# A fused involution and mixture-of-experts kernel on one core: the last group's routing done in a row, and the last scatters put behind the additions

## The chip, the cores and the metric

The kernel runs on one core of one Trainium2 chip. The metric is the time of one execution in device microseconds (us); lower is better. The engines are TensorE (PE, with its weight loads PEld), VectorE (DVE), ScalarE (ACT), GpSimd (POOL) and SyncE (SP, which here only issues transfers). Each works through its own list of instructions strictly in the order in which they are written, and waits on semaphores where the program says so.

## The reference

```python
x = x + conv(_ln_c(x))            # x: 4 x 128 x 56 x 56
#   h    = reduce_w @ x + reduce_b       (128 -> 32 channels)
#   kern = span_w @ h + span_b           (49 taps x 16 groups, each pixel has its own)
#   conv = sum over 49 taps of kern * shifted x
t = tokens of x                   # 12544 tokens of 128 channels
t = t + ffn(_ln_t(t))
#   probs = softmax(t @ router_w.T), the best 2 of 8 experts, their shares made to sum to 1
#   y_e   = w2[e] @ (silu(w1[e] @ t) * (w3[e] @ t))      128 -> 341 -> 128
#   ffn   = sum over a token's 2 experts of share * y_e
```

## The kernel before, in words

The work has two halves that overlap. The **convolution** runs over 28 tiles of 448 pixels (8 image rows), each in 25 steps of one or two taps: TensorE makes the per-pixel kernels in `kern_ps` (L586), VectorE multiplies them with the shifted input (L851), and GpSimd (L1088) and TensorE (L601) add up the products. The **experts' half** takes finished tokens. Tiles are gathered in 15 groups (two tiles each, then tile 26 alone and tile 27 alone). For a group, VectorE does the `route` (19 small operations: best two experts, shares), TensorE the `rank` (running counts, L564 and L567), VectorE the `place` (4 operations: each token's row, `slots`) and the `table` (16 operations: which expert and rows each block of 512 tokens has). GpSimd then scatters each token's row twice into `xs` in DRAM, in order of experts: 8 indirect transfers per tile (L1097). When all scatters of a group have landed, the group's **blocks** of 512 rows can be loaded. There are 56 blocks. Block b needs: a load of its rows `xb` (L485) and of its expert's weights (L494, L499) from SyncE; a transpose X(b) on TensorE (L573), copied out by ScalarE and VectorE; six matmul slots of the hidden layer (L623, L624, L627), with silu on ScalarE and a product `hid` on VectorE; three thirds of the second layer (L536, 24 matmuls in all), called y(b) here; a copy `y_tok` on ScalarE (L685); and four indirect **additions** into `out` by GpSimd (L1109). The first addition of a block waits until all four of the block before have landed (`s_add`), since two blocks may hold the same token.

What sets the order is a table of numbers worked out when the program is built. Each engine's code is a loop over steps S, and a step number says in which step each piece of work stands. The convolution ends at S = 700; blocks 31 to 55 are added after it. A group's routing is written as offsets from `ROUTER_AT[g]` (for the last group, 700): `ROUTE_OFF`, `RANK_OFF`, `PLACE_OFF`, `TABLE_OFF`. The scatters stand in `SCATTER_AT`, behind each other, during the convolution only in the steps of a tile that `SCATTER_J` lists, and after it one in every step. A group's blocks may start at `READY` (its last scatter's step plus `LANDING`, 5 steps). From `READY` follow the steps of the slots, of X (`X_AT`), of y (`Y_AT`), of the loads (`LOAD_AT`) and of the additions (`ADD_AT`). The PSUM tile `bank` is shared by X, y, the router's logits and the rank, one use after another in order of their steps, so a use that waits holds up all uses behind it. Blocks 35 to 37 are those of the group of tiles 24 and 25, 38 and 39 those of tile 26, and 40 to 55 those of tile 27. The first load of a group (block 35, 38 or 40) waits for the group's last scatter to have landed (L478), and block 40's also for the eight `pad` transfers (L466), which fill each expert's last block with empty rows.

The load of a block and the wait of the group's first block:

```python
if b == BLOCK0[g]:
    sp.wait_ge(s_tab, TABLES.index(g) + 1)
    ...
        sp.wait_ge(s_scat[i], 16 * 2 * SUBS * tiles)
    if g == NG - 1:
        sp.wait_ge(s_pad, 16 * EXPERTS)
```

Of the kernel before, what the change touches and what calls it, by code (L numbers as in the profile page):

```python
# [23 lines left out]
TILES = B * PER_IMG  # L24
# [17 lines left out]
LATE = 8  # L42
# [34 lines left out]
CONV_END = TILES * TAPS  # L77
# [5 lines left out]
LANDING = 5  # L83


def at(p, j):
    return p * TAPS + j
# [3 lines left out]
J_STAT1, J_RSTD1, J_NORM1, J_XN, J_H = 0, 4, 6, 9, 21  # L91

PIECE_J = (3, 4, 5, 7, 8, 10, 12)
SCATTER_J = [(1, 5, 9, 11, 13, 15, 17, 19, 21, 23) if t < LATE else (1, 4, 7, 10, 13, 16, 19, 22, 24) for t in range(TILES)]
ADD_J = (0, 2, 5, 8, 11, 14, 17, 20, 23)


ROUTE_OFF = (19, 19, 19, 21, 21, 21, 21, 23, 23, 23, 25, 25, 25, 29, 29, 31, 31, 31, 31)
RANK_OFF = 26
PLACE_OFF = (27, 27, 29, 29)  # L100
TABLE_OFF = (33, 33, 33, 35, 35, 35, 35, 37, 37, 37, 37, 39, 39, 39, 41, 41)
EXP_OFF, GATES_OFF = 24, 32

ROUTER_AT = [at(tiles[-1] + 1, 0) for tiles in GROUPS_OF]
SCATTER_AT = {}
READY = []
_free = FIRST
for _g, _tiles in enumerate(GROUPS_OF):
    _S = max(_free, ROUTER_AT[_g] + PLACE_OFF[-1] + 1)
    _items = [(t, q, k) for t in _tiles for q in range(SUBS) for k in range(2)]  # L110
    while _items:
        if _S >= CONV_END or _S % TAPS in SCATTER_J[_S // TAPS]:
            SCATTER_AT[_S] = _items.pop(0)
        _S += 1
    _free = _S
    READY.append(max(_S + LANDING, ROUTER_AT[_g] + TABLE_OFF[-1] + 4))

SLOT_AT = []
_S, _acc = 0, 0
for _b in range(NBLOCKS):  # L120
    _S = max(_S, READY[BATCH_OF[_b]] + 7)
# [11 lines left out]


TAKEN = {at(_t - 1, j) for _t in range(TILES) for j in (J_XN, J_H)} | {at(_t + 1, j) for _t in range(TILES) for j in (J_XN2, J_LG)}
TAKEN |= {S + RANK_OFF for S in ROUTER_AT}

X_AT, Y_AT, LOAD_AT, ADD_AT = {}, {}, {}, {}
_x = []
for _b in range(NBLOCKS):  # L140
    _ready = READY[BATCH_OF[_b]]
    _S = max(_ready + 3, SLOT_AT[(_b - 2) * SLOTS + 5] if _b >= 2 else 0)
    if _b < 2:
        _S = max(_S, SLOT_AT[_b * SLOTS] - 4)
# [8 lines left out]
    _n = 3 if _y < CONV_END else 1  # L153
# [3 lines left out]
    assert _y not in Y_AT and (not _b or _y > _x[-1][1])  # L157
    Y_AT[_y] = _b
    _x.append((_S, _y))
_add = 0  # L160
for _b in range(NBLOCKS):
    _ready = READY[BATCH_OF[_b]]
    LOAD_AT.setdefault(max(_ready - 2, _x[_b][0] - 8), []).append(("x", _b))
    LOAD_AT.setdefault(max(_ready - 1, SLOT_AT[(_b - 2) * SLOTS + 5] + 1 if _b >= 2 else 0), []).append(("w", _b))
    LOAD_AT.setdefault(max(_ready, _x[_b - 2][1] + 1 if _b >= 2 else 0), []).append(("w2", _b))
    for _q in range(BSUBS):
        _add = max(_add, _x[_b][1] + 2)
        while _add < CONV_END and (_add % TAPS not in ADD_J or _add in ADD_AT):
# [15 lines left out]
    BANK_AT.setdefault(_S, []).append(("y", _b))  # L184

for _g in range(NG):
    BANK_AT.setdefault(ROUTER_AT[_g] + RANK_OFF, []).append(("rank", _g))
BANK_NO = {}
for _S in sorted(BANK_AT):
    for _use in BANK_AT[_S]:  # L190
# [24 lines left out]
for _t in range(TILES):  # L215
    _S = at(_t, J_X1 + 1)
# [21 lines left out]
def build(nc, x, w_red, b_red, w_span, router, w13, w2, ident, lower, consts, tabs, ids, empty, out):  # L238
    with ExitStack() as ctx:  # L239
# [190 lines left out]
        def _(sp):  # L430
# [70 lines left out]
            for S in range(FIRST, END):  # L501
                p, j = divmod(S, TAPS)
                if j == 12 and p >= 0 and p < WPIECES:
                    load_raw(p)
                if j == 20 and p >= 0 and p < WPIECES:
                    store_w(p)
                if j == J_X1 + 1 and 1 <= p <= TILES:
                    t = p - 1
                    sp.wait_ge(s_x1, t + 1)
                    sp.dma_start(token_rows(out, t), x1[:, t % 3]).then_inc(s_spill[t % 3], 16)  # L510
                    if t + 4 < TILES:
                        sp.dma_start(xt[:, t % 4], token_rows(x, t + 4)).then_inc(s_xin[t % 4], 16)
                if S == ROUTER_AT[NG - 1] + TABLE_OFF[-1] + 1:
                    pad()
                for what, b in LOAD_AT.get(S, []):
                    load_block(what, b)
# [131 lines left out]
        def _(act):  # L648
# [115 lines left out]
            for S in range(FIRST, END):  # L764
                p, j = divmod(S, TAPS)
                if p == -1 and j in PIECE_J:
                    i = PIECE_J.index(j)
                    act.wait_ge(s_span_in[i], 16)
                    act_f(span[:, i * SCOLS:(i + 1) * SCOLS], prod[0:98, i, 0:SCOLS], ACT.Copy).then_inc(s_piece_hi, 1)
                if j == 14 and 0 <= p < WPIECES:  # L770
                    act.wait_ge(s_wraw_in, 16 * (p + 1))
                    if p >= 2:
                        act.wait_ge(s_wstore, 16 * (p - 1))
                    act_f(wb[:, p % 2, :, 0, :], w_raw[:], ACT.Copy).then_inc(s_whi, 1)
                if S in MOE_AT and MOE_AT[S] % 2 == 0:
# [12 lines left out]
                if J_NORM1 <= j < J_NORM1 + 2 and p + 1 < TILES:
                    normalise("ln1", p + 1, j - J_NORM1)
                if J_NORM2 <= j < J_NORM2 + 2 and 0 <= p - 1 < TILES:  # L790
                    normalise("ln2", p - 1, j - J_NORM2)
                if j == J_NORM2 + 4 and 0 <= p - 1 < TILES:
                    twin(p - 1)
                for g in range(NG):
                    if S == ROUTER_AT[g] + EXP_OFF:
                        exponentials(g)
                    if S == ROUTER_AT[g] + GATES_OFF:
                        gates(g)

        @block.vector  # L800
        def _(dve):
# [204 lines left out]

            def routing(S):
                for g in range(NG):
                    for k, off in enumerate(ROUTE_OFF):
                        if S == ROUTER_AT[g] + off:  # L1010
                            route(g, k)
                    for k, off in enumerate(PLACE_OFF):
                        if S == ROUTER_AT[g] + off:
                            place(g, k)
                    for k, off in enumerate(TABLE_OFF):
                        if BATCH[g] and S == ROUTER_AT[g] + off:
                            table(g, k)

            def hidden(n):
# [6 lines left out]
            for S in range(FIRST, END):  # L1026
# [20 lines left out]
                if j == J_X1 and 0 <= p - 1 < TILES:  # L1047
                    t = p - 1
# [12 lines left out]
        def _(pool):  # L1061
# [121 lines left out]
```

## Time and profile before

| | |
|---|---|
| median of 3 runs | 1503.39 us (1500.45 to 1503.68) |
| the profiled execution, its own time | 1498.94 us |
| its span, first to last instruction | 1497.1 us |
| busy: PE, PEld, DVE, ACT, POOL | 1243.9, 1015.6, 1122.8, 579.5, 1112.2 us |
| mean granted clock of TensorE | 0.95 of full speed |

Busy time is the sum of an engine's instructions; an engine can be waited for without being busy, and a busy one need not be waited for. The shares are means over a convolution of some 1200 us and a stretch behind it of some 290 us, which have different limits; the change is about the passage from one to the other. The times in the rows below are us from the span's start.

### The profile page before, as it was taken

What the parts mean: (1) busy time and instruction counts of PE and PEld (TensorE: products, weight loads), DVE (VectorE), ACT (ScalarE), POOL (GpSimd) and SP (SyncE); (2) the same over time, 40 slices, a digit from 0 to 9 for tenths busy, and PEclk for the clock granted to TensorE, in tenths of its full rate; (3) what the DMA queues carried; (4) which work ended last, traced back from release to release, by engine and by line L of the source; (5) the groups of instructions that cost most, each with busy time, mean ns of one, the idle gap of its engine ahead of it and who ended that gap; (6) DMA issues with size and microseconds to landing.
All of it is one profiled execution on the core that took longest, in us unless ns stands there. A gap on an engine that the chain in (4) does not pass through costs nothing. (4 is left out here: it accounts for less than half of the span.)

```text
span 1497.1 us, 23125 instructions
## 1 busy us (share of the span) xinstructions
PE 1243.9 (83%) x7667; PEld 1015.6 (68%) x7667; DVE 1122.8 (75%) x1663; ACT 579.5 (39%) x1960; POOL 1112.2 (74%) x788
## 2 busy tenths in 40 slices
PE   4898878788988989899899898899989887587771
PEld 2676767676766777677787777777778676465661
DVE  5998888988898998888889898888889943222220
ACT  4333333334443444444345343454434244133230
POOL 4787979784686887678788687877778875665665
PEclk9999898998999999999999999999999999899996
DMA  4111111112232242332324232243322445666652
GB/s 124 41 60 48 59 49 59 49 31 88 53 79 60 69 97 63 88 78 60 85 59 103 62 86 62 60 100 83 71 58 48 105 119 129 174 137 134 145 117 25
DMA packets 93346, 120.40 MB, mean 80 GB/s; under 512 B 11531, under 2 KB 72428, under 8 KB 93082
## 3 DMA queue, kind: packets, MB, share of 16 engines
q1 hardware_dynamic: 53802, 90.97, 20.0%
q0 software_dynamic: 39424, 27.96, 13.3%
q8 instruction: 61, 1.00, 0.3%
q14 instruction: 59, 0.48, 0.1%
HBM read 78.92 MB, written 42.65 MB: 81 GB/s over the span
## 5 line engine op out<-in xcount | busy, mean ns | idle before, releaser
L851 DVE TENSOR_TENSOR prod<-kern_ps,xn 128x896 f32<-128x896 f32 x592 | 627.9, 1082 | 65.7 <-PE kern_ps L586 63.2
L586 PE MATMUL kern_ps<-h_stack,span 98*128 98x448 f32 x1372 | 466.3, 426 | 112.7 <-DVE prod L851 72.1
L1088 POOL TENSOR_TENSOR acc_p<-acc_p,prod 128x896 f32<-128x896 f32 x192 | 435.9, 2270 | 74.1 <-DVE prod L851 69.4
L1109 POOL DMA_INDIRECT out<-y_tok,idx x224 | 351.6, 1570 | 137.4 <-issue 66.2
L601 PE MATMUL acc_ps<-ident_sb,prod 128*112 128x128 f32 x2864 | 388.4, 280 | 0.0
L601 PEld LDWEIGHTS acc_ps<-ident_sb,prod 128*112 128x112 f32 x2864 | 341.3, 137 | 37.9 <-DVE x L1053 7.8
L586 PEld LDWEIGHTS kern_ps<-h_stack,span 98*128 98x128 f32 x1372 | 227.1, 200 | 205.5 <-DVE prod L851 121.5
L1097 POOL DMA_INDIRECT xs<-rows_x,slots x224 | 219.0, 978 | 61.0 <-issue 41.3
L536 PEld LDWEIGHTS bank<-w2b,hid 114*128 114x128 f32 x1344 | 181.7, 202 | 50.7 <-DVE xf_lo L1046 26.0
L536 PE MATMUL bank<-w2b,hid 114*128 114x128 f32 x1344 | 190.1, 288 | 26.2 <-DVE xf_lo L1046 15.9
L780 ACT ACTIVATE silu<-h_ps 114x512 f32<-114x512 f32 x132 | 79.0, 598 | 235.0 <-PE h_ps L627 235.0
L1024 DVE TENSOR_TENSOR hid<-silu,h_ps 114x512 f32<-114x512 f32 x132 | 89.9, 681 | 97.9 <-ACT silu L780 68.8
L623 PE MATMUL h_ps<-xf_hi,wb 128*114 128x512 f32 x264 | 118.5, 449 | 15.3 <-ACT silu L780 13.6
L1084 POOL TENSOR_TENSOR acc_p<-prod 128x896 f32<-128x896 f32 x28 | 62.9, 2247 | 85.9 <-DVE prod L851 52.2
L685 ACT ACTIVATE y_tok<-bank,xb 128x128 f32<-128x128 f32 x224 | 64.1, 373 | 118.6 <-PE bank L536 98.1
L627 PE MATMUL h_ps<-xf_lo,wb 128*114 128x512 f32 x264 | 106.1, 402 | 0.0
L624 PE MATMUL h_ps<-xf_hi,wb 128*114 128x512 f32 x264 | 105.9, 401 | 0.0
L845 DVE TENSOR_TENSOR kern_ps<-kern_ps,xn 128x896 f32<-128x896 f32 x80 | 87.2, 1090 | 12.3 <-PE kern_ps L586 11.4
L848 DVE TENSOR_TENSOR prod<-kern_ps,prod 128x896 f32<-128x896 f32 x80 | 87.3, 1091 | 2.8
L1024 DVE TENSOR_TENSOR hid<-silu,kern_ps 114x512 f32<-114x512 f32 x36 | 24.7, 685 | 84.2 <-ACT silu L780 63.1
L1074 POOL TENSOR_TENSOR rstd_ln<-veps_ln,minus_half 112x4 f32<-112x4 f32 x56 | 67.0, 1196 | 15.0 <-ACT veps_ln L718 14.9
L755 ACT ACTIVATE rows_x<-x,shift_ln,rstd_ln 112x128 f32<-112x128 f32 x112 | 47.8, 485 | 56.4 <-POOL shift_ln L1076 56.3
(154 smaller groups left out, 1349.9 us busy)
## 6 DMA issues: line engine op xcount, KB each, us to landing
wb<-wexp SPq DMA_DIRECT2D x56, 684.0 KB, 5.4
xb<-xs SPq DMA_DIRECT2D x56, 264.0 KB, 3.0
w2b<-in_w SPq DMA_DIRECT2D x56, 171.0 KB
xt<-in_x SPq DMA_DIRECT2D x28, 224.0 KB, 3.4
out<-x SPq DMA_DIRECT2D x28, 224.0 KB, 2.6
wexp<-wb SPq DMA_DIRECT2D x8, 684.0 KB, 3.2
xs<-rows_x,slots POOLq DMA_INDIRECT x224, 2.3
out<-y_tok,idx POOLq DMA_INDIRECT x224
```

The lines of the kernel that those rows point to most:

```text
L536: i = mm(bank[:, k * C:(k + 1) * C], hid[:, (CPE * b + c) % HR, k * 128:(k + 1) * 128], w2b[:, b % 2, c, :], start=c == 0 and k == 0, stop ...
L586: last = mm(kern_ps[:, g % 2, i, 0:N], span[:, k * C:(k + 1) * C], h_stack[:, t % 2, :], start=True, stop=True)
L601: last = mm(acc_ps[0:SUB, k * C:(k + 1) * C], src[:, at_:at_ + SUB], ident_sb[:], is_transpose=True, start=u == BY_PE[t][0] and i == 0 and ...
L623: mm(ps, lo, xf_hi[:, b % 2, :], start=True, stop=False)
L624: mm(ps, hi, xf_hi[:, b % 2, :], start=False, stop=False)
L627: mm(ps, hi, xf_lo[:, b % 2, :], start=False, stop=True).then_inc(done, 1)
L848: v.tensor_tensor(dst.rearrange("p (i n) -> p i n", i=2), kern, prod[:, (g - 1) % PRING, :].rearrange("p (i n) -> p i n", i=2), ALU.add).t ...
L851: v.tensor_tensor(pair_rows(dst), kern.rearrange("p i (r w) -> p i r w", w=W), taps, ALU.mult).then_inc(s_prod, 1)
L1024: v.tensor_tensor(hid[:, n % HR, :], silu[:, n % 2, :], h_at(n, 1), ALU.mult).then_inc(s_hid, 1)
L1088: g_.tensor_tensor(acc_p[:], acc_p[:], prod[:, (t * TAPS + u) % PRING, :], ALU.add).then_inc(s_padd, 1)
L1097: g_.indirect_dma_start(out=xs, out_offset=bass.IndirectOffsetOnAxis(ap=slots[:, k, n:n + 1], axis=0), in_=rows_x[:, t % XN2RING, q, k, :] ...
L1109: g_.indirect_dma_start(out=out, out_offset=bass.IndirectOffsetOnAxis(ap=idx[:, b % XBRING, q:q + 1], axis=0), in_=y_tok[:, b % 2, q * C:( ...
```

## The change

It has four parts. The last group (tile 27) gets a table of offsets of its own, `LAST_OFF`: route at steps 718 and 720, rank and exponentials at 719, place at 720, gates and table at 721, where before they stood between 719 and 741. In the last tile of the convolution scatters may stand in 12 steps instead of 9. The scatters that are left at step 700 (22; before, 25) lose their own steps and are issued behind the fourth addition of blocks 31 to 37, by `SCATTERS_BEHIND`; the plan's `READY` is still worked out from their former steps, so the blocks move up: X(38) from step 732 to 729, X(40) from 748 to 741, the program's end from 855 to 851. A load of `xb` now keeps its order, and the first one of a late group is planned 4 steps ahead of X instead of 8. The eight pads move from step 742 to 722.

```diff
-SCATTER_J = [(1, 5, 9, 11, 13, 15, 17, 19, 21, 23) if t < LATE else (1, 4, 7, 10, 13, 16, 19, 22, 24) for t in range(TILES)]
+SCATTER_J = [(1, 5, 9, 11, 13, 15, 17, 19, 21, 23) if t < LATE else (1, 4, 7, 10, 13, 16, 19, 22, 24) if t < TILES - 1 else
+             (1, 4, 6, 9, 10, 12, 15, 16, 18, 19, 22, 24) for t in range(TILES)]
...
+LAST_OFF = {"route": (18,) * 13 + (20,) * 6, "rank": 19, "exp": 19, "place": (20,) * 4, "gates": 21, "table": (21,) * 16}
...
-    _S = max(_free, ROUTER_AT[_g] + PLACE_OFF[-1] + 1)
+    _S = max(_free, ROUTER_AT[_g] + off(_g, "place")[-1] + 1)
...
-    LOAD_AT.setdefault(max(_ready - 2, _x[_b][0] - 8), []).append(("x", _b))
+    _lead = 4 if _b and _b == BLOCK0[BATCH_OF[_b]] and _ready > CONV_END else 8
+    _load = max(_ready - 2, _x[_b][0] - _lead, _load)
+    LOAD_AT.setdefault(_load, []).append(("x", _b))
...
+SCATTERS_BEHIND = [4, 3, 3, 3, 3, 3, 4]
+BEHIND = {}
+_tail = [SCATTER_AT.pop(S) for S in sorted(SCATTER_AT) if S >= CONV_END]
+for _S in sorted(ADD_AT):
+    if _S >= CONV_END and _tail:
+        _n = SCATTERS_BEHIND.pop(0)
+        BEHIND[ADD_AT[_S][-1][0]], _tail = _tail[:_n], _tail[_n:]
...
                 for b, q in ADD_AT.get(S, []):
                     add_rows(b, q)
+                    if q == BSUBS - 1:
+                        for item in BEHIND.get(b, []):
+                            scatter(*item)
```

`off(g, what)` gives `LAST_OFF` for the last group and the former tables for all others.

On GpSimd, from tile 27's first scatter (the row that waits for `s_spill0`) to block 36's additions, before. L1097 is a scatter, L1109 an addition:

```order
L1097 DMA xs<-rows_x,slots 104960x132 [waits s_twin,s_spill0,s_gates,s_slots]
L1097 DMA xs<-rows_x,slots 104960x132
L1109 DMA out<-y_tok,idx 13056x128 [waits s_add,s_idx,s_bank_out]
L1109 DMA out<-y_tok,idx 13056x128 x3
L1097 DMA xs<-rows_x,slots 104960x132 x6
L1109 DMA out<-y_tok,idx 13056x128 [waits s_add,s_idx,s_bank_out]
L1109 DMA out<-y_tok,idx 13056x128 x3
```

And there, now, from block 35's additions to the last scatter; scatters are L1121, additions L1133:

```order
L1133 DMA out<-y_tok,idx 13056x128 [waits s_add,s_idx,s_bank_out]
L1133 DMA out<-y_tok,idx 13056x128 x3
L1121 DMA xs<-rows_x,slots 104960x132
L1121 DMA xs<-rows_x,slots 104960x132 [waits s_twin,s_spill0,s_gates,s_slots]
L1121 DMA xs<-rows_x,slots 104960x132
L1133 DMA out<-y_tok,idx 13056x128 [waits s_add,s_idx,s_bank_out]
L1133 DMA out<-y_tok,idx 13056x128 x3
L1121 DMA xs<-rows_x,slots 104960x132 x3
L1133 DMA out<-y_tok,idx 13056x128 [waits s_add,s_idx,s_bank_out]
L1133 DMA out<-y_tok,idx 13056x128 x3
L1121 DMA xs<-rows_x,slots 104960x132 x3
```

The eight scatters of tile 27 stood in a 2 and a 6 ahead of the additions of blocks 35 and 36. Now the first two stand behind block 35's additions, three behind block 36's and the last three behind block 37's; tile 26's last one stands first behind block 35's.

On TensorE, around X(40) (the matmuls with `xb`), before. The slots are L623, L624 and L627, the thirds L536; the third here is the last one of y(38):

```order
L623 MATMUL h_ps<-xf_hi,wb 114x512 [waits s_silu]
L624 MATMUL h_ps<-xf_hi,wb 114x512
L627 MATMUL h_ps<-xf_lo,wb 114x512
L536 MATMUL bank<-w2b,hid 128x128 [waits s_hid]
L536 MATMUL bank<-w2b,hid 128x128 x3
L623 MATMUL h_ps<-xf_hi,wb 114x512 [waits s_hid]
L624 MATMUL h_ps<-xf_hi,wb 114x512
L627 MATMUL h_ps<-xf_lo,wb 114x512
L573 MATMUL bank<-ident_sb,xb 128x128 [waits s_xb0,s_bank_out]
L573 MATMUL bank<-ident_sb,xb 128x128 x3
```

And there, now (L647 to L651 the slots, L597 the transpose, L560 the thirds); the third here is the first one of y(38):

```order
L647 MATMUL h_ps<-xf_hi,wb 114x512 [waits s_hid]
L648 MATMUL h_ps<-xf_hi,wb 114x512
L651 MATMUL h_ps<-xf_lo,wb 114x512
L597 MATMUL bank<-ident_sb,xb 128x128 [waits s_xb0,s_bank_out]
L597 MATMUL bank<-ident_sb,xb 128x128 x3
L647 MATMUL kern_ps<-xf_hi,wb 114x512 [waits s_silu,s_xf_hi,s_wb1]
L648 MATMUL kern_ps<-xf_hi,wb 114x512
L651 MATMUL kern_ps<-xf_lo,wb 114x512 [waits s_bank_out]
L560 MATMUL bank<-w2b,hid 128x128 [waits s_hid,s_w2b0,s_bank_out]
L560 MATMUL bank<-w2b,hid 128x128 x3
```

X(40) stood behind the last third of y(38), and now stands ahead of its first. X(35) still stands ahead of y(34), and X(38) ahead of y(36); the last group's logits, which stood ahead of X(35), now stand behind it.

## Rows read from the trace of the kernel before

**Rows 1.** The page: span, and the chain that ended last by line

```profile
span 1497.1 us, 23125 instructions
...
POOL out L1109 7%; DMA out<-y_tok,idx 5%; POOL xs L1097 0%; ACT idx L680 0%; POOLq L239 0%; POOLq L1106 0%
```

**Rows 2.** Windows: busy us by engine, then clock, DMA share, GB/s

```profile
1300.00:1311.00 11.00, 8.72 (x45) 7.26 (x46) 2.07 (x3) 1.89 (x4) 4.66 (x3) 0.81 0.84 217
...
1331.80:1383.50 51.70, 39.73 (x231) 30.05 (x232) 13.47 (x21) 16.67 (x46) 31.04 (x20) 1.00 0.63 140
```

**Rows 3.** GpSimd's timeline: start, us, line; a first addition unless L1097 or L1074

```profile
1212.78 1.59 POOL L1109 DMA_INDIRECT out<-y_tok,idx  x1 [2.30 <-ACT y_tok L685]
...
1224.03 0.94 POOL L1097 DMA_INDIRECT xs<-rows_x,slots  x1 [0.30 <-issue]
1225.00 1.05 POOL L1074 TENSOR_TENSOR rstd_ln<-veps_ln,minus_half 112x4 f32<-112x4 f32 x1
...
1229.49 1.61 POOL L1109 DMA_INDIRECT out<-y_tok,idx  x1 [0.30 <-issue]
...
1272.12 1.60 POOL L1109 DMA_INDIRECT out<-y_tok,idx  x1 [0.31 <-issue]
...
1279.59 0.97 POOL L1097 DMA_INDIRECT xs<-rows_x,slots  x1 [0.30 <-issue]
...
1287.11 1.60 POOL L1109 DMA_INDIRECT out<-y_tok,idx  x1 [0.30 <-issue]
...
1311.88 1.55 POOL L1109 DMA_INDIRECT out<-y_tok,idx  x1 [6.30 <-ACT idx L680]
...
1331.79 1.55 POOL L1109 DMA_INDIRECT out<-y_tok,idx  x1 [2.48 <-ACT idx L680]
...
1483.42 1.55 POOL L1109 DMA_INDIRECT out<-y_tok,idx  x1 [2.43 <-DMA out<-y_tok,idx]
```

**Rows 4.** Chain of waits, blocks 38 to 40: start, us, what

```profile
1304.02 7.08 DMA out<-y_tok,idx
...
1337.36 3.65 DMA out<-y_tok,idx
```

**Rows 5.** SyncE's timeline: loads xb, wb; the eight pads

```profile
1227.44 1.51 SPq L485 DMA_DIRECT2D xb<-xs  x2
...
1283.66 9.69 SPq L466 DMA_DIRECT2D xs<-in_empty  x8
...
1297.87 1.48 SPq L485 DMA_DIRECT2D xb<-xs  x2
```

**Rows 6.** TensorE's timeline

```profile
1208.38 2.94 PE L536 MATMUL bank<-w2b,hid 114*128 114x128 f32 x24 [0.23 <-DVE base L938]
...
1235.41 0.95 PE L559 MATMUL bank<-router_sb,xn 128*112 128x8 f32 x8
...
1300.60 1.09 PE L573 MATMUL bank<-ident_sb,xb 128*128 128x128 f32 x4 [11.68 <-DMA xb<-xs]
...
1313.39 0.66 PE L573 MATMUL bank<-ident_sb,xb 128*128 128x128 f32 x4
...
1315.47 1.16 PE L536 MATMUL bank<-w2b,hid 114*128 114x128 f32 x8 [0.72 <-DVE xf_lo L1046]
...
1318.74 1.05 PE L536 MATMUL bank<-w2b,hid 114*128 114x128 f32 x8
```

**Rows 7.** ScalarE's timeline

```profile
1211.36 1.15 ACT L685 ACTIVATE y_tok<-bank,xb 128x128 f32<-128x128 f32 x4 [2.58 <-PE bank L536]
...
1250.26 0.23 ACT L725 ACTIVATE lexp<-ldiff 112x32 f32<-112x32 f32 x1
```

**Rows 8.** VectorE's timeline

```profile
1240.65 0.18 DVE L880 TENSOR_REDUCE small_sb<-hit 112x4 f32<-112x32 f32 x1
...
1241.30 0.19 DVE L888 SCALAR_TENSOR_TENSOR wide_sb<-hot,wide_sb 112x32 f32<-112x32 f32 x1
```

**Rows 9.** Tile xs: transfers from issue to landing

```profile
DMA to landing us min/median/max: 2.3/3.4/6.4
```

More of the change, by code:

```diff
@@ L102, with off @@
 EXP_OFF, GATES_OFF = 24, 32
+LAST_OFF = {"route": (18,) * 13 + (20,) * 6, "rank": 19, "exp": 19, "place": (20,) * 4, "gates": 21, "table": (21,) * 16}
+def off(g, what):
+    if g == NG - 1:
+        return LAST_OFF[what]
+    return {"route": ROUTE_OFF, "rank": RANK_OFF, "exp": EXP_OFF, "place": PLACE_OFF, "gates": GATES_OFF, "table": TABLE_OFF}[what]
 ROUTER_AT = [at(tiles[-1] + 1, 0) for tiles in GROUPS_OF]
@@ L115 @@
     _free = _S
-    READY.append(max(_S + LANDING, ROUTER_AT[_g] + TABLE_OFF[-1] + 4))
+    READY.append(max(_S + LANDING, ROUTER_AT[_g] + off(_g, "table")[-1] + 4))
 SLOT_AT = []
@@ L135 @@
 TAKEN = {at(_t - 1, j) for _t in range(TILES) for j in (J_XN, J_H)} | {at(_t + 1, j) for _t in range(TILES) for j in (J_XN2, J_LG)}
-TAKEN |= {S + RANK_OFF for S in ROUTER_AT}
+TAKEN |= {S + off(g, "rank") for g, S in enumerate(ROUTER_AT)}
 X_AT, Y_AT, LOAD_AT, ADD_AT = {}, {}, {}, {}
@@ L159 @@
     _x.append((_S, _y))
-_add = 0
+_add = _load = 0
 for _b in range(NBLOCKS):
     _ready = READY[BATCH_OF[_b]]
-    LOAD_AT.setdefault(max(_ready - 2, _x[_b][0] - 8), []).append(("x", _b))
+    _lead = 4 if _b and _b == BLOCK0[BATCH_OF[_b]] and _ready > CONV_END else 8
+    _load = max(_ready - 2, _x[_b][0] - _lead, _load)
+    LOAD_AT.setdefault(_load, []).append(("x", _b))
     LOAD_AT.setdefault(max(_ready - 1, SLOT_AT[(_b - 2) * SLOTS + 5] + 1 if _b >= 2 else 0), []).append(("w", _b))
@@ L171 @@
 END = max(max(ADD_AT), max(X_AT), max(Y_AT)) + 3
+SCATTERS_BEHIND = [4, 3, 3, 3, 3, 3, 4]
[5 more added lines that the diff above has]
+        BEHIND[ADD_AT[_S][-1][0]], _tail = _tail[:_n], _tail[_n:]
+assert not _tail and all(len({b for b, _ in ADD_AT[S]}) == 1 for S in ADD_AT)
 BANK_AT = {}
@@ L186 @@
 for _g in range(NG):
-    BANK_AT.setdefault(ROUTER_AT[_g] + RANK_OFF, []).append(("rank", _g))
+    BANK_AT.setdefault(ROUTER_AT[_g] + off(_g, "rank"), []).append(("rank", _g))
 BANK_NO = {}
@@ L512, in _ @@
                         sp.dma_start(xt[:, t % 4], token_rows(x, t + 4)).then_inc(s_xin[t % 4], 16)
-                if S == ROUTER_AT[NG - 1] + TABLE_OFF[-1] + 1:
+                if S == ROUTER_AT[NG - 1] + off(NG - 1, "table")[-1] + 1:
                     pad()
@@ L794, in _ @@
                 for g in range(NG):
-                    if S == ROUTER_AT[g] + EXP_OFF:
+                    if S == ROUTER_AT[g] + off(g, "exp"):
                         exponentials(g)
-                    if S == ROUTER_AT[g] + GATES_OFF:
+                    if S == ROUTER_AT[g] + off(g, "gates"):
                         gates(g)
@@ L1008, in routing @@
                 for g in range(NG):
-                    for k, off in enumerate(ROUTE_OFF):
-                        if S == ROUTER_AT[g] + off:
+                    for k, steps in enumerate(off(g, "route")):
+                        if S == ROUTER_AT[g] + steps:
                             route(g, k)
-                    for k, off in enumerate(PLACE_OFF):
-                        if S == ROUTER_AT[g] + off:
+                    for k, steps in enumerate(off(g, "place")):
+                        if S == ROUTER_AT[g] + steps:
                             place(g, k)
-                    for k, off in enumerate(TABLE_OFF):
-                        if BATCH[g] and S == ROUTER_AT[g] + off:
+                    for k, steps in enumerate(off(g, "table")):
+                        if BATCH[g] and S == ROUTER_AT[g] + steps:
                             table(g, k)
```

## The prediction

> **What bounds the kernel now.** I read the page first. The chain that ended last runs almost only over GpSimd's additions (L1109) and their landing [rows 1], so I read the end of the kernel from GpSimd's timeline. The first addition of block 31 stands at 1212.78, that of block 40 at 1331.79, that of block 55 at 1483.42 [rows 3]. Blocks 40 to 55 are evenly spaced: (1483.42 − 1331.79)/15 = 10.1 us. Blocks 31 to 40 take 119.0/9 = 13.2 us each. Only these nine intervals, 28 us above the even pace, are in the change's reach.
>
> The even interval is a wait for a landing. From 1272.12 to the scatter at 1279.59 four additions take 7.47 us to issue [rows 3]. The last addition lands 3.65 us after its issue [rows 4], and 0.8 us later the next block starts: 5.6 + 3.65 + 0.8 = 10.1. GpSimd is free for the last 2.6 us of each interval. TensorE is busy for 39.7 of 51.7 us there [rows 2] and does not set the pace.
>
> The nine slow intervals hold scatters. Six of them take 1287.11 − 1279.59 = 7.52 us, 1.25 each [rows 3], and they stand ahead of the additions whatever the additions wait for: block 35 to 36 takes 15.0 us. Intervals with scatters are issue-bound, those without are landing-bound.
>
> **What the change removes.** An interval with three scatters behind the additions takes 7.47 + 3.75 = 11.2 us: 2.6 us of the scatters are hidden in the landing. Block 31 carries four scatters and the normalisation's two small operations, which last from 1225.00 to about 1227 [rows 3]. That gives 7.47 + 5.0 + 2.0 = 14.5, where it was 16.7. If nothing else waited: block 32 at 1227.2, block 37 at 1227.2 + 5 × 11.2 = 1283.2, block 38 at 1294.4, and without scatters block 40 at 1314.6. That is 17.2 us earlier than 1331.79.
>
> The three more scatters inside the convolution cost GpSimd 3.8 us. They are covered: the additions of block 31 wait 2.30 us for `y_tok` [rows 3], and those of the convolution run ahead of their readers. Uncovered, the price is at most 1.5 us.
>
> **What it adds.** Each late group's last scatter is now issued later, with additions ahead of it, and three things hang on it in series: its landing, the load of `xb`, and X, which holds the shared `bank` ahead of the y of the block two before. That y is needed by the next additions. I price the links:
> - scatter's issue to the load's issue: 1224.03 [rows 3] to 1227.44 [rows 5], 3.4 us
> - load's issue to X: 1297.87 [rows 5] to 1300.60 [rows 6], 2.7 us
> - X to the end of y: 1313.39 to 1318.74 + 1.05 [rows 6], 6.4 us; `y_tok` ends 1.5 us later (0.3 and the 1.15 of [rows 7]): 7.9 us in all
> - clock: after its 11.68 us of idleness TensorE ran X(40) in 1.09 us instead of 0.66 [rows 6], and the granted clock was 0.81 over the next 11 us against 1.00 in the even stretch [rows 2]. I add 1.3 us per long wait.
>
> By the Trainium skill (TensorE: Matmul & The Clock Gate, "What's actually happening") an idle array falls to 1.2 GHz and activity releases the throttle. If all of the 6.4 us ran at that level, it would add 6 us instead of 1.3; 0.81 says that only a part does.
>
> *X(35)* hangs on tile 25's last scatter, now second behind block 32's additions: issued at 1227.2 + 7.47 + 1.25 = 1235.9, load at 1239.3 (was 1227.44), X at 1242.0. The last group's logits (L559, 1235.41 before [rows 6]) now stand behind it. From X: bank free after 2.1 (1313.39 to 1315.47 [rows 6]), logits 0.95 and their copy 0.2, then 13 route operations in a row. Four of these took 1241.30 + 0.19 − 1240.65 [rows 8], 0.21 each, so 13 take 2.8: 6.1 us. Then X(36), exponentials with two table loads, six more route operations and two of place until the bank is free: I take 4 us, an estimate between 1.7 (8 × 0.21) and 6. Then y(34), 2.94 like y(31) [rows 6], and 1.5: block 34's additions at X + 14.7 = 1256.7. Free of this they would start at 1249.6, so 7.1 us are lost.
>
> The row of routing itself gains nothing on the path: it makes the tables ready some 20 us early, while the last scatters come later. The table's 16 operations (16 × 0.21 = 3.4 us) delay two `hid` products; block 35's additions, due at 1267.9, cover that.
>
> *X(38)*: tile 26's last scatter stands first behind block 35's additions: 1256.7 + 11.2 = 1267.9, scatter at 1275.4, load 1278.8, X at 1281.5, y(36) and `y_tok` with the clock's share 9.2: block 36 at 1290.7 instead of 1279.1, 11.6 us lost. The pads (9.69 us on SyncE [rows 5]) now stand ahead of this load, from about 1259 to 1269. They end before the scatter lands, so they cost nothing; if the scatter came early, the load could not be issued before about 1270.
>
> *X(40)*: block 37 at 1290.7 + 11.2 = 1301.9. Tile 27's last scatter is third behind it: 1301.9 + 7.47 + 2.5 = 1311.9, load 1315.3, X at 1318.0. Before, X(40) waited too, 11.68 us, at no price, since y(38) stood ahead of it. Now y(38) is behind: block 38's additions at 1318.0 + 9.2 = 1327.2 (were 1311.88 [rows 3]), instead of 1301.9 + 11.2 = 1313.1: 14.1 us lost.
>
> **The sum.** 7.1 + 11.6 + 14.1 = 32.8 lost against 17.2 won: +15.6. Block 40 at 1327.2 + 20.2 = 1347.4; from there on nothing changes. The profiled execution (1498.94; span 1497.1 [rows 1]) would become 1514.5. It ran 4.5 us below the median of the runs shown, 1503.39, which would become 1519.
>
> The Trainium skill (DMA: Bandwidth & Descriptors, "Rules for kernel authors") says to issue a DMA early, compute, and wait on its semaphore late. The change puts these scatters later and their readers earlier. If each load were issued 8 us earlier, as the rule would have it, most of the 32.8 us would not arise and the sum would be negative.
>
> **Rivals.**
> 1. *The other side: the waits stay short and the hiding wins* (1 in 10). For it: the 17.2 us are read directly from intervals, and X(40)'s wait was free before. Against it: the order on TensorE. The mechanism is that TensorE is itself late, so that X(38) and X(40) find their rows there. It decides where the three losses together fall under 17.2 us, about half of what I found. Fully so, 1503.4 − 17.2 = 1486.
> 2. *Landings are slow* (1 in 8). Beside loads an addition took 7.08 us to land [rows 4], and transfers of `xs` up to 6.4 us against 3.4 in the middle [rows 9]. With 3.0 us more at each of three scatters and 2.2 us more on each interval before blocks 33, 35 and 37 (5.6 + 7.08 + 0.8 = 13.4 for 11.2), less what a stall absorbs, some 11 us more: 1530.
> 3. *The losses are partly absorbed* (1 in 12). If the part I took as 4 us is 1.7 and no clock is lost, and y(36) or y(38) come 2 us sooner each, 9 us fall away: 1510.
> 4. *No net effect* (1 in 25): gains and losses cancel, 1503.
>
> **How the numbers follow.** My own case holds about 0.65, from 1511 to 1527: it is the sum with its loose terms (4 us between 1.7 and 6; the clock's 1.3 between 0 and 6, twice; scatter landing between 2.3 and 4.5). The range 1508 to 1529 adds rival 3 and part of rival 2 and leaves out the faster side. A measurement here tells about 0.2% (3 us) from no change. Slower: my case, rivals 2 and 3, 0.86. Same 0.04, faster 0.10.
>
> **What would show it.** In the profile after: `xb` loads of blocks 35, 38 and 40 at about 1239, 1279 and 1315; TensorE idle ahead of X(38) and X(40) for some 15 us each, released by the landing of `xb`; additions of blocks 36 and 38 waiting for `y_tok` and not for a landing; first additions of blocks 34, 36, 38 and 40 at about 1257, 1291, 1327 and 1347; the last 15 intervals still 10.1 us. Wrong it would be if X(38) found its rows waiting, or if the additions of blocks 32 to 37 stood 11.2 us apart throughout.

## The result, and the profile after

The changed kernel took 1521.94 us (median of 4 runs, 1520.93 to 1525.14), the kernel before 1503.54 (4 runs, 1500.45 to 1505.34): a ratio of 1.0128, 95% interval 1.0105 to 1.0151. It is slower, by 18.4 us where the forecast said 15.6, and inside the range of 1508 to 1529.

The profiled execution took 1525.14 us. The page of the changed kernel, its span and the chain that ended last by engine:

```profile
span 1523.3 us, 23125 instructions
...
PE 39%; DVE 24%; POOL 14%; issue 12%; DMA 5%; ACT 4%; SPq 0%; DVEq 0%; POOLq 0%; ACTq 0%
```

These shares can't be held against those of before: there the chain is followed only through the additions [rows 1], here on through the convolution. From 1220 us on, the same view by line:

```profile
by line: POOL out L1133 37.5%; DMA out<-y_tok,idx 19.7%; issue 15.1%; PE bank L560 5.3%; POOL xs L1121 3.6%; DMA xb<-xs 2.7%; DMA xs<-rows_x,slots 2.3%; PE bank L597 1.7%; ACT idx L704 1.1%; ACT xf_hi L701 0.9%; ACT y_tok L709 0.9%; DVE xf_
```

The additions and their landings still lead. But y (L560), the scatters' landing (`xs`) and the landing of `xb` are now links of the chain. Before, over the same stretch, none of them but the scatters' issue was:

```profile
by line: POOL out L1109 37.0%; DMA out<-y_tok,idx 26.6%; issue 15.2%; POOL xs L1097 2.3%; ACT idx L680 1.2%; POOLq L239 0.7%; POOLq L1106 0.1%
```

The place to read is again GpSimd's timeline. The columns are start, duration, line and operation, and in brackets the idle time before and what ended it. L1133 is an addition, here the first one of blocks 31, 32, 34, 35, 36, 38 and 40; L1121 is a scatter (tile 26's last one at 1284.68, tile 27's last one at 1321.27):

```profile
1218.73 1.60 POOL L1133 DMA_INDIRECT out<-y_tok,idx  x1 [8.76 <-ACT y_tok L709]
...
1232.88 1.62 POOL L1133 DMA_INDIRECT out<-y_tok,idx  x1 [0.55 <-issue]
...
1265.69 1.59 POOL L1133 DMA_INDIRECT out<-y_tok,idx  x1 [10.53 <-ACT y_tok L709]
...
1277.22 1.59 POOL L1133 DMA_INDIRECT out<-y_tok,idx  x1 [0.54 <-issue]
...
1284.68 0.97 POOL L1121 DMA_INDIRECT xs<-rows_x,slots  x1 [0.30 <-issue]
...
1299.96 1.59 POOL L1133 DMA_INDIRECT out<-y_tok,idx  x1 [11.79 <-ACT y_tok L709]
...
1321.27 0.94 POOL L1121 DMA_INDIRECT xs<-rows_x,slots  x1 [0.30 <-issue]
1336.90 1.59 POOL L1133 DMA_INDIRECT out<-y_tok,idx  x1 [14.69 <-ACT y_tok L709]
...
1359.35 1.54 POOL L1133 DMA_INDIRECT out<-y_tok,idx  x1 [4.83 <-ACT idx L704]
```

Block 31 to block 32 took 14.2 us and block 34 to block 35 11.5 us, as the hiding of the scatters promised. The first additions of blocks 34, 36 and 38 waited 10.5, 11.8 and 14.7 us for `y_tok`. Block 31 to block 40 took 1359.35 − 1218.73 = 140.6 us, before 1331.79 − 1212.78 = 119.0 [rows 3]: 21.6 us more. From there to block 55 the intervals are 10.0 us each, as even as before.

SyncE's timeline shows the loads of `xb` for blocks 35, 38 and 40 (L509) and the eight pads (L490):

```profile
1245.20 0.36 SPq L509 DMA_DIRECT2D xb<-xs  x1
...
1265.73 10.29 SPq L490 DMA_DIRECT2D xs<-in_empty  x8
...
1288.11 0.33 SPq L509 DMA_DIRECT2D xb<-xs  x1
...
1324.62 0.33 SPq L509 DMA_DIRECT2D xb<-xs  x1
```

TensorE's timeline shows X(35) (L597), the last group's logits (L583), the 24 matmuls of y(34) (L560), and X(38) and X(40) (L597):

```profile
1248.29 1.09 PE L597 MATMUL bank<-ident_sb,xb 128*128 128x128 f32 x4 [6.25 <-DMA xb<-xs]
...
1250.78 1.66 PE L583 MATMUL bank<-router_sb,xn 128*112 128x8 f32 x8
...
1258.74 5.49 PE L560 MATMUL bank<-w2b,hid 114*128 114x128 f32 x24 [0.34 <-DVE base L962]
...
1290.86 1.09 PE L597 MATMUL bank<-ident_sb,xb 128*128 128x128 f32 x4 [16.15 <-DMA xb<-xs]
...
1327.28 1.09 PE L597 MATMUL bank<-ident_sb,xb 128*128 128x128 f32 x4 [18.41 <-DMA xb<-xs]
```

X(35), X(38) and X(40) stood for 6.25, 16.15 and 18.41 us, released by the landing of `xb`. Before, of these only X(40) waited for its rows, 11.68 us [rows 6]. The logits took 1.66 us where they took 0.95, and y(34) 5.49 us where y(31) took 2.94 [rows 6].

Three windows of the changed kernel, in the columns of [rows 2] (the granted clock stands third from the end):

```profile
1250.00:1264.00 14.00, 13.31 (x53) 10.43 (x51) 10.86 (x46) 5.08 (x11) 4.24 (x4) 0.50 0.47 137
1309.00:1327.00 18.00, 0.00 (x0) 0.00 (x0) 0.66 (x1) 0.00 (x0) 10.77 (x9) 0.59 0.29 49
1331.80:1383.50 51.70, 45.37 (x269) 35.98 (x267) 15.78 (x24) 20.43 (x52) 27.41 (x18) 0.99 0.62 140
```

From 1250 to 1264, the stretch of the logits and y(34), the granted clock was 0.50, the lower of TensorE's two levels (1.2 of 2.4 GHz). In the 18 us ahead of X(40) TensorE did nothing at all. In the third window, the same stretch of time as the one of before, it was busy for 45.37 us instead of 39.73, with work that had stood earlier before.

Of the chain of waits of the changed kernel, three links (start, us, what): the landing of tile 27's last scatter, of block 40's `xb`, and of block 39's last addition:

```profile
1321.27 2.31 DMA xs<-rows_x,slots
...
1324.62 2.52 DMA xb<-xs
...
1352.98 5.60 DMA out<-y_tok,idx
```

### The profile page after: what moved, and what is told of

It reads as the page before. It is cut to its first block, busy times and chain, and to the rows that moved or that the text cites. A ratio compares the mean times of both kernels' runs of the same rounds, so it can differ in the third digit from the quotient of the medians.

```text
span 1523.3 us, 23125 instructions
## 1 busy us (share of the span) xinstructions
PE 1256.5 (82%) x7667; PEld 1029.8 (68%) x7667; DVE 1124.4 (74%) x1663; ACT 580.8 (38%) x1960; POOL 1112.5 (73%) x788
## 4 chain that ended last, share of the span: by engine, by line
PE 39%; DVE 24%; POOL 14%; issue 12%; DMA 5%; ACT 4%; SPq 0%; DVEq 0%; POOLq 0%; ACTq 0%
PE acc_ps L625 13%; PE kern_ps L610 11%; DVE prod L875 11%; POOL out L1133 8%; PE bank L560 7%; DMA out<-y_tok,idx 4%; DVE kern_ps L869 4%; POOL acc_p L1112 3%; PE h_ps L647 2%; PE h_ps L648 2%; PE h_ps L651 2%; DVE hid L1048 2%; DVE prod L872 2%; POOL xs L1121 1%; POOL rstd_ln L1098 1%
## 5 line engine op out<-in xcount | busy, mean ns | idle before, releaser
L1133 POOL DMA_INDIRECT out<-y_tok,idx x224 | 351.4, 1569 | 167.5 <-issue 59.3
L625 PE MATMUL acc_ps<-ident_sb,prod 128*112 128x128 f32 x2864 | 393.3, 282 | 0.0
L625 PEld LDWEIGHTS acc_ps<-ident_sb,prod 128*112 128x112 f32 x2864 | 345.5, 138 | 38.2 <-DVE x L1077 7.8
L1121 POOL DMA_INDIRECT xs<-rows_x,slots x224 | 219.6, 980 | 55.5 <-issue 35.6
L560 PEld LDWEIGHTS bank<-w2b,hid 114*128 114x128 f32 x1344 | 185.8, 206 | 50.3 <-DVE xf_lo L1070 25.2
L560 PE MATMUL bank<-w2b,hid 114*128 114x128 f32 x1344 | 194.5, 293 | 24.5 <-DVE xf_lo L1070 13.6
L647 PE MATMUL h_ps<-xf_hi,wb 128*114 128x512 f32 x264 | 120.5, 456 | 10.4 <-ACT silu L804 7.6
L651 PE MATMUL h_ps<-xf_lo,wb 128*114 128x512 f32 x264 | 107.2, 406 | 0.0
L648 PE MATMUL h_ps<-xf_hi,wb 128*114 128x512 f32 x264 | 107.1, 406 | 0.0
L1070 DVE TENSOR_TENSOR xf_lo<-bank,xf_hi 128x512 fp32r<-128x512 f32 x56 | 38.4, 686 | 57.9 <-ACT xf_hi L701 57.8
```

The costliest lines, as they stand in the source:

```text
L560: i = mm(bank[:, k * C:(k + 1) * C], hid[:, (CPE * b + c) % HR, k * 128:(k + 1) * 128], w2b[:, b % 2, c, :], start=c == 0 and k == 0, stop ...
L625: last = mm(acc_ps[0:SUB, k * C:(k + 1) * C], src[:, at_:at_ + SUB], ident_sb[:], is_transpose=True, start=u == BY_PE[t][0] and i == 0 and ...
L647: mm(ps, lo, xf_hi[:, b % 2, :], start=True, stop=False)
L648: mm(ps, hi, xf_hi[:, b % 2, :], start=False, stop=False)
L651: mm(ps, hi, xf_lo[:, b % 2, :], start=False, stop=True).then_inc(done, 1)
L1121: g_.indirect_dma_start(out=xs, out_offset=bass.IndirectOffsetOnAxis(ap=slots[:, k, n:n + 1], axis=0), in_=rows_x[:, t % XN2RING, q, k, :] ...
```

## The experiments

All ran in five rounds beside the kernel before on the same chip, whose median was 1500.8 to 1501.2 us there. Beside each ratio stands how long the profiled execution took from the first addition of block 31 to that of block 40 (31→40), and to that of block 55 (31→55). The kernel before took 119.0 and 270.6 us, the changed kernel 140.6 and 291.0. Each such pair is from one execution, the ratio from several.

**1. X(38) and X(40) planned behind the y's.** Of the changed kernel, only the plan's places of two X, and of the loads that go by them, are later: X(38) behind y(36), X(40) behind y(38).

```diff
+    if _b in (38, 40):
+        _S = max(_S, _x[_b - 2][1] + 1)
     while _S in TAKEN:
         _S += 1
```

> The changed kernel with X(38) planned behind y(36) and X(40) behind y(38); scatters, routing and pads as changed. Theory (the order on TensorE turns the late scatters' landing into a wait of the additions): block 36 follows block 35 after 11.2 us instead of 22.7, block 38 follows 37 after 11.2 instead of 25.7; part comes back one block later, since X(38) still comes late for y(37) (2.5 us) and X(40) for y(39) (7 us). Net 14 to 18 us faster than the changed kernel, so about 1506, within 4 us of the kernel before. Rival (scatters behind additions slow the additions' queue itself, whatever TensorE does): within 3 us of the changed kernel, 1522.

It took 1507.76 us, ratio 1.0046 (1.0028 to 1.0065); 31→40 125.9, 31→55 279.7 us. About two thirds of the loss are gone with two numbers of a plan. GpSimd's timeline, first additions of blocks 36 to 39, and below it TensorE's, the first slot of the hidden layer for block 37:

```profile
1287.51 1.59 POOL L1135 DMA_INDIRECT out<-y_tok,idx  x1 [3.46 <-ACT y_tok L711]
...
1300.89 1.59 POOL L1135 DMA_INDIRECT out<-y_tok,idx  x1 [2.43 <-ACT y_tok L711]
...
1312.16 1.59 POOL L1135 DMA_INDIRECT out<-y_tok,idx  x1 [0.30 <-issue]
...
1329.95 1.54 POOL L1135 DMA_INDIRECT out<-y_tok,idx  x1 [10.64 <-ACT y_tok L711]
```

```profile
1278.47 0.77 PE L649 MATMUL kern_ps<-xf_hi,wb 128*114 128x512 f32 x1 [8.12 <-DMA wb<-wexp]
```

Block 36 follows 35 after 14.4 us where it was 22.7, block 38 follows 37 after 11.3 where it was 25.7. Something is left at both places. Block 36 isn't at 11.2; by the rows it is because block 37's slots waited 8.12 us for weights whose load stands behind the pads on SyncE (no run moved the pads in this kernel). And block 39 now takes 17.8 us, since X(40) waits 10.34 us ahead of y(39).

**2. X(35) behind y(34) too.** The last experiment, and the group of tiles 24 and 25, with all blocks behind it, planned 8 steps later.

```diff
+READY[12] += 8
 SLOT_AT = []
```

> As the run before, and the steps of blocks 35 to 55 moved 8 later in the plan, so that on TensorE the last group's logits, the rank and y(34) stand ahead of X(35). Theory: block 34's additions start 22.4 us after block 32's instead of 32.8, of which X(35), now late for y(35), takes back 1 to 3 us: 6 to 9 us faster than the run before, about 1499. Rival: the 10 us before block 34 are the row of routing operations, not X(35): no faster than the run before.

It took 1511.46 us, ratio 1.0065 (1.0042 to 1.0088); 31→40 128.0, 31→55 283.6 us. The expected gain didn't come. First additions of blocks 32, 34 and 35 on GpSimd, the pads and the load of block 37's `xb` on SyncE, and X(37) on TensorE:

```profile
1226.23 1.62 POOL L1137 DMA_INDIRECT out<-y_tok,idx  x1 [0.55 <-issue]
...
1250.84 1.59 POOL L1137 DMA_INDIRECT out<-y_tok,idx  x1 [2.36 <-ACT idx L708]
...
1273.53 1.59 POOL L1137 DMA_INDIRECT out<-y_tok,idx  x1 [11.72 <-ACT y_tok L713]
```

```profile
1248.01 10.11 SPq L494 DMA_DIRECT2D xs<-in_empty  x8
...
1260.26 0.54 SPq L513 DMA_DIRECT2D xb<-xs  x1
```

```profile
1264.89 1.09 PE L601 MATMUL bank<-ident_sb,xb 128*128 128x128 f32 x4 [7.53 <-DMA xb<-xs]
```

Block 34 now follows block 32 after 24.6 us instead of 32.8: X(35) did cost 8 us. But block 35 follows after 22.7 us instead of 11.5. The load of block 37's `xb` is issued at 1260.26, behind 10.11 us of pads, and X(37) holds the bank ahead of y(35) as X(35) did ahead of y(34). The same mechanism has moved from X(35) to X(37), with SyncE's queue in the scatter's place.

**3. The pads out of the way.** Experiment 2, with the pads at step 736 instead of 722.

```diff
-                if S == ROUTER_AT[NG - 1] + off(NG - 1, "table")[-1] + 1:
+                if S == 736:
```

> The second experiment's kernel (X(35) behind y(34), X(38) behind y(36), X(40) behind y(38)) with the pads moved on SyncE from step 722 to 736, behind the loads of blocks 36 and 37. Theory: there block 35 stood 22.7 us behind block 34 because SyncE issued block 37's rows only after the pads (10.1 us), and X(37) stands ahead of y(35); with the pads behind it block 35 follows after 11.3 to 13, so 9 to 11 us faster than that kernel, about 1501. Rival: X(35) itself is late for y(35) and the pads only filled the wait: within 3 us of that kernel.

It took 1505.49 us, ratio 1.0028 (1.0010 to 1.0046); 31→40 119.6, 31→55 275.6 us. Block 34 to block 35 fell from 22.7 to 14.4 us. The mechanism was right, its size smaller than expected: about 6 of the 9 to 11 us arrived, and the blocks behind took some of it back (17.0 us ahead of block 39).

**4. Only the pads later.** The changed kernel with the pads at step 731.

> The changed kernel with only the pads moved, from step 722 to 731, behind the loads for blocks 38 and 39. The prediction's claim: the pads cost nothing in the changed kernel, since X(38) waits longer than they delay anything. Then within 3 us of the changed kernel. Rival: they take SyncE 10.3 us ahead of block 37's weights, and y(36) or the landing of additions pays 3 us or more: faster by that.

It took 1519.33 us, ratio 1.0123 (1.0106 to 1.0140); 31→40 142.3, 31→55 293.5 us. In the changed kernel the pads cost nothing that shows, as the prediction had it. They cost some 6 us (experiment 2 against 3) once the scatters' wait above them is taken away. The 3 us that experiment 1 lacks at block 36 are put down to them by its rows alone.

**5. Only the routing in a row.** The changed kernel with the scatters in their own steps, 9 steps in the last tile, and all loads 8 steps ahead: `LAST_OFF` is what is left, and with it the pads' place and the loads' order.

```diff
-_tail = [SCATTER_AT.pop(S) for S in sorted(SCATTER_AT) if S >= CONV_END]
+_tail = []
...
-    _lead = 4 if _b and _b == BLOCK0[BATCH_OF[_b]] and _ready > CONV_END else 8
+    _lead = 8
```

> The kernel before with only the last group's routing in a row (and with it the pads and the last scatters' steps earlier, which stand ahead of the additions of blocks 34 and 35 as steps of their own); no scatters behind additions, nine scatter steps in the last tile. Theory (the row of routing costs nothing and pays where the scatters keep their steps): block 35 about the same, block 36 some 6 us earlier, block 38 and all after it 8 to 12 us earlier than before: about 1493. Rival (the row of 13, 10 and 16 operations on VectorE holds up the slots): 1503 or slower.

It took 1495.32 us, ratio 0.9958 (0.9942 to 0.9973); 31→40 112.8, 31→55 263.2 us. This part alone is a gain.

**6. All but the routing in a row.** The changed kernel in which `off` gives the former tables for the last group too.

```diff
-    if g == NG - 1:
-        return LAST_OFF[what]
```

> The changed kernel with the last group's routing at its former offsets; scatters behind additions as changed. X(40) then stands behind y(38) again by its step (748 against 747), X(38) still ahead of y(36), X(35) ahead of y(34). Theory: the wait before block 36 stays (22.7 us after block 35), the one before block 38 is gone but X(40) comes some 6 us late for y(39): 6 to 10 us faster than the changed kernel, about 1514. Rival (the loss lies in the scatters behind the additions, the routing in a row is a gain on top): slower than the changed kernel, above 1525.

It took 1516.88 us, ratio 1.0100 (1.0080 to 1.0119); 31→40 132.9, 31→55 288.6 us. The loss is there without the routing in a row. It is 0.28% smaller than in the changed kernel, with intervals that overlap. On GpSimd, a scatter of tile 27 and block 39's first addition:

```profile
1297.17 0.96 POOL L1119 DMA_INDIRECT xs<-rows_x,slots  x1 [15.38 <-issue]
...
1341.41 1.54 POOL L1131 DMA_INDIRECT out<-y_tok,idx  x1 [12.06 <-ACT y_tok L707]
```

The scatter waited 15.38 us for the shares that it writes, which ScalarE makes behind X(38). Here the ring of waits closes on GpSimd itself: scatters wait for X, and X for scatters ahead of them.

**7. Only the twelve steps.** The kernel before, with 12 instead of 9 steps for scatters in the last tile.

```diff
-... (1, 4, 7, 10, 13, 16, 19, 22, 24) for t in range(TILES)]
+... (1, 4, 7, 10, 13, 16, 19, 22, 24) if t < TILES - 1 else
+             (1, 4, 6, 9, 10, 12, 15, 16, 18, 19, 22, 24) for t in range(TILES)]
```

> The kernel before with only the twelve scatter steps in the convolution's last tile (three scatters more inside it, three fewer behind it). The prediction's claim: at most 1.5 us lost inside the convolution, covered; behind it three scatters fewer stand ahead of block 32's additions, which are issue-bound: 2 to 4 us earlier there, of which the landings give back a part. Between 3 us faster and 1 us slower than before. Rival: GpSimd falls behind and VectorE waits for it: 4 us or more slower.

It took 1493.14 us, ratio 0.9951 (0.9932 to 0.9970); 31→40 112.1, 31→55 261.3 us. The gain is larger than expected. On GpSimd, the first addition of block 35, the scatter behind its fourth, and block 36's first:

```profile
1263.63 1.55 POOL L1110 DMA_INDIRECT out<-y_tok,idx  x1 [4.18 <-ACT idx L681]
...
1271.04 0.97 POOL L1098 DMA_INDIRECT xs<-rows_x,slots  x1 [0.30 <-issue]
...
1277.32 1.60 POOL L1110 DMA_INDIRECT out<-y_tok,idx  x1 [0.30 <-issue]
```

Before, two scatters of tile 27 stood ahead of block 35's additions and held them 5.40 us for the shares (L1097 at 1269.58). With three scatters fewer the plan puts them behind these additions, and block 35 starts at 1263.63 instead of 1272.12 [rows 3]. I hadn't counted that a scatter fewer can also take a wait out of the additions' way. The convolution doesn't pay for it: block 31 starts at 1213.56 against 1212.78.

**8. Each X behind the last y of the group before.** X(35) behind y(34), X(38) behind y(37), X(40) behind y(39), pads at step 736.

```diff
+READY[12:] = [719, 745, 765]
...
-                if S == ROUTER_AT[NG - 1] + off(NG - 1, "table")[-1] + 1:
+                if S == 736:
```

> The changed kernel with scatters behind additions and routing in a row kept, but each late group's steps moved so far that its first X stands behind the last y of the group before (X(35) behind y(34), X(38) behind y(37), X(40) behind y(39)), and the pads at step 736. Theory: every wait for late rows is then covered by additions already computed; blocks 31 to 38 follow after 14.1 and six times 11.3, block 39 and 40 after 10.1: block 40 at 102 us after block 31 instead of 119, so 15 to 18 us faster than the kernel before, about 1485. Rival (the late scatters cost by themselves): X(40) comes too late for y(40) however it stands, and no more than 5 us are won.

It took 1496.76 us, ratio 0.9962 (0.9947 to 0.9977); 31→40 114.0, 31→55 269.3 us. This keeps the scatters where the change put them and is faster than the kernel before, but has only about a quarter of the expected gain (4.0 us of 15 to 18). On GpSimd, the first additions of blocks 35, 37 and 39, and two links of the chain, block 36's last addition and block 41's `xb`:

```profile
1265.70 1.59 POOL L1135 DMA_INDIRECT out<-y_tok,idx  x1 [3.65 <-ACT y_tok L711]
...
1290.64 1.59 POOL L1135 DMA_INDIRECT out<-y_tok,idx  x1 [2.35 <-DMA out<-y_tok,idx]
...
1315.71 1.54 POOL L1135 DMA_INDIRECT out<-y_tok,idx  x1 [6.65 <-DMA out<-y_tok,idx]
```

```profile
1282.97 6.88 DMA out<-y_tok,idx
...
1306.60 5.63 DMA xb<-xs
```

Block 35 still waits 3.65 us for y; the waits ahead of blocks 37 and 39 are now for landings. An addition landed in 3.65 us in the even stretch [rows 4], and in 6.88 here. Loads held back behind a scatter are issued together, and the additions land beside them. That they cause the slow landings is argued from the rows; no run took the loads away.

**9. Only the scatters back in their own steps.** The changed kernel with one part undone: routing in a row and twelve steps stay.

```diff
-_tail = [SCATTER_AT.pop(S) for S in sorted(SCATTER_AT) if S >= CONV_END]
+_tail = []
```

> The changed kernel with one part undone: no scatters behind additions, each of the 22 left ones in a step of its own; routing in a row, twelve steps in the last tile and the earlier pads kept. Theory (the whole loss is the scatters' late place): the three waits for late rows are gone, and the gains of the two other parts, measured alone at 0.42% and 0.49%, add in part: 0.6 to 0.9% faster than the kernel before, about 1490. Rival: the order on TensorE that the earlier plan brings (X(40) ahead of y(38)) costs even with early scatters: within 3 us of the kernel before.

It took 1491.91 us, ratio 0.9935 (0.9911 to 0.9958); 31→40 112.3, 31→55 261.5 us. It has the lowest ratio of all, though its interval overlaps those of experiments 5, 7, 8 and 10. GpSimd, first additions of blocks 31 and 40, and X(38) on TensorE:

```profile
1213.62 1.60 POOL L1133 DMA_INDIRECT out<-y_tok,idx  x1 [2.53 <-ACT y_tok L709]
...
1325.89 1.55 POOL L1133 DMA_INDIRECT out<-y_tok,idx  x1 [3.42 <-ACT idx L704]
```

```profile
1272.41 1.08 PE L597 MATMUL bank<-ident_sb,xb 128*128 128x128 f32 x4 [9.78 <-DMA xb<-xs]
```

X(38) still waits 9.78 us, on its load behind the pads, and the additions of block 36 behind it waited only 3.08.

**10. Behind the additions, but early.** The changed kernel, the same 22 scatters behind five blocks instead of seven.

```diff
-SCATTERS_BEHIND = [4, 3, 3, 3, 3, 3, 4]
+SCATTERS_BEHIND = [6, 4, 4, 4, 4, 0, 0]
```

> The changed kernel with the 22 scatters behind additions as 6, 4, 4, 4, 4 behind blocks 31 to 35 instead of 4, 3, 3, 3, 3, 3, 3 behind 31 to 37; all else as changed, X(38) ahead of y(36) and X(40) ahead of y(38) too. Theory (only the time at which a group's last scatter stands matters, not the hiding): tile 25's last stands behind block 31, tile 26's behind 33, tile 27's behind 35, each some 11 to 23 us earlier, so no X waits; intervals 17, 12.5 four times, then about 10.5: block 40 at 108 to 111 us after block 31, 0.5 to 0.7% faster than the kernel before. Rival: scatters behind additions cost by themselves: slower than the kernel before.

It took 1493.44 us, ratio 0.9941 (0.9917 to 0.9964); 31→40 113.4, 31→55 262.3 us. First additions of blocks 31 and 40:

```profile
1218.78 1.60 POOL L1133 DMA_INDIRECT out<-y_tok,idx  x1 [8.72 <-ACT y_tok L709]
...
1332.18 1.54 POOL L1133 DMA_INDIRECT out<-y_tok,idx  x1 [3.27 <-ACT idx L704]
```

One list of seven numbers takes the changed kernel from 1.28% slower to 0.59% faster. Scatters behind additions aren't the fault. The last one was issued at 1321.27, and here at 1284.27. The intervals with four scatters take 12.5 us instead of 11.2 and are still the better bargain. The time came as expected, the stretch to block 40 some 2 us longer than the 108 to 111.

## Why the prediction was right

**The mechanism** was the predicted one and is shown from both sides: with the X moved behind the y's two thirds of the loss go (experiment 1) or all of it (8), and with the last scatters earlier all of it goes (9 and 10). Rival 1, that TensorE would be late itself and the hiding win, fell: it would have had to find its rows waiting, and found them 16 and 18 us late. Rivals 3 and 4 fell too: no part of the three losses was absorbed, and the gain of the hiding didn't make up for them.

**The price of each part**, from first addition to first addition:

| from block to block | predicted | measured |
|---|---|---|
| 31 to 32 | 14.5 | 14.2 |
| 32 to 34, with X(35) | 29.5 | 32.8 |
| 34 to 35 | 11.2 | 11.5 |
| 35 to 36, with X(38) | 22.8 | 22.7 |
| 36 to 37 | 11.2 | 11.3 |
| 37 to 38, with X(40) | 25.3 | 25.7 |
| 38 to 40 | 20.2 | 22.4 |
| sum, 31 to 40 | 134.6 | 140.6 |

*The hiding* is real: 11.3 us for an interval with three scatters, 11.2 forecast. *X(38) and X(40)* came as worked out, scatter by scatter: X(38) 13.6 us after block 35's first addition and the next additions 9.1 behind X (9.2 forecast), X(40) 16.1 after block 37's and 9.6 behind.

**Two terms were too small.** The first is X(35) to block 34's additions, taken as 14.7 us and measured 1265.69 − 1248.29 = 17.4. I took the logits at 0.95 us and y(34) "like y(31)" at 2.94, and added no clock; at 0.50 of full speed they took 1.66 and 5.49. (The parts as I wrote them add up to 14.5, not 14.7.) I had overlooked that the trace of the kernel before has a row for y(34) itself. Its first 16 matmuls, and the window over their start:

```profile
1240.79 3.78 PE L536 MATMUL bank<-w2b,hid 114*128 114x128 f32 x16 [1.41 <-DVE xf_lo L1046]
```

```profile
1240.00:1243.00 3.00, 2.21 (x10) 2.21 (x11) 1.35 (x5) 0.22 (x2) 2.37 (x3) 0.50 0.59 194
```

With the 1.27 us of the other eight that is 5.05 us for the 24 matmuls, at a granted clock of 0.50 at their start. Read from there instead of from y(31), the term would have been 2.1 us larger. The 4 us that I had called loose were right or a little high: logits and y alone make up 3.3 us, more than the whole difference of 2.7. The second is the 20.2 us from block 38 to 40, taken from the even pace. Block 39's last addition landed in 5.60 us instead of 3.65. This is rival 2 in small: its 2.2 us came at one interval, not on all.

**The three more scatters in the convolution** cost nothing that can be told from chance. The changed kernel's block 31 started 5.95 us later than before, but the same code up to there started it at 1214.58 in experiment 4, and at 1218.78 in experiment 10. With nine steps, it started at 1212.78 before and at 1216.81 in experiment 5, again with the same code up to there. Executions of one code differ by some 4 us in the convolution. That is one reason why the median moved by 18.4 us and the profiled span by 26.2; another is that the profiled execution of the kernel before, at 1498.94 us, was faster than its four runs, and that of the changed kernel the slowest of its four. The forecast of 15.6 us is best held against the stretch that the change touches: 31→55 moved by 20.3.

**The row of routing, which "itself gains nothing on the path"**: right for this kernel, whose last scatters come later than the tables (with the former tables it is no slower, experiment 6). What it is worth elsewhere the prediction did not ask: 0.4% alone (experiment 5). The effects don't simply add: routing −0.42%, twelve steps −0.49%, both −0.65%, with intervals that overlap.

**Left open:** why experiments 3 and 8 lack some 4 and 12 us of what was expected of them (slow landings beside bunched loads fit the rows and weren't tried alone), and what sets the 4 us between executions in the convolution.

## What to carry to other kernels

Work that is put behind something else on an in-order queue is cheap only until its last reader is due: follow the last item of each group, not the sum (here scatter, load, transpose, shared bank, an earlier block's result), and issue that item early even if a few others then stand uncovered. When items move by a table, move their readers' places in the plan as well; a plan worked out from the old places puts a waiting instruction ahead of work that was ready. After a wait is removed, look at what it covered: here eight pads that had cost nothing took some 6 us.

## What the runs showed of the hardware

The lower clock lasts on when TensorE works again. In the changed kernel it was 0.50 over 14 us in which TensorE was busy for 13.31, and the 24 matmuls of y(34) took 5.49 us, against the 2.94 of y(31). X(35) waited 6.25 us ahead of it, but experiment 9 has the same 5.49 us without such a wait: from 1235 to 1240 the clock there was 0.96, and from 1235 on nothing ahead of y(34) waited longer than 1.95. Its y(34) on TensorE, and the windows ahead of it and over it:

```profile
1246.52 5.49 PE L560 MATMUL bank<-w2b,hid 114*128 114x128 f32 x24 [0.83 <-DVE base L962]
```

```profile
1240.00:1246.50 6.50, 3.75 (x25) 2.54 (x24) 5.20 (x25) 4.87 (x9) 5.58 (x4) 0.93 0.70 178
1246.50:1252.00 5.50, 5.48 (x25) 5.48 (x26) 4.49 (x21) 0.00 (x0) 1.55 (x1) 0.50 0.27 24
```

In the 6.5 us ahead TensorE was busy for 3.75, in short pieces, at 0.93; over y(34) it was busy for 5.48 of 5.50 us, at 0.50. So here only a stretch of short waits stood between the higher clock and the fall, and the fall is seen on the work behind it. By the Trainium skill (TensorE: Matmul & The Clock Gate, "What's actually happening") an idle array falls to the lower level and activity releases it. The trace agrees with both: behind its 16.15 us of idleness X(38) took 1.09 us instead of 0.66, and the three thirds of y(36) behind it 1.97, 1.05 and 1.05; but the release can come late, as over y(34).

The last of a block's four additions landed 3.65 us after its issue in the even stretch, and 5.60 to 7.08 us after it in three cases in which loads of rows or weights were issued within 2 us of it (in the changed kernel at 1353.54 and 1354.64, beside the addition at 1352.98). By the Trainium skill (DMA: Bandwidth & Descriptors, "Queues, rings and completion order") each DMA engine takes turns between the queues it has work for, which would let such loads slow an addition; no run here shows the turns themselves.
